# The order of GpSimd's and VectorE's steps around the fp6 quantisers of a transformer-mamba kernel

## The reference, cut to what matters

```python
x = x + attention(layernorm(x), Wqkv, Wproj)          # x: 16 x 1024 x 256, fp32
x = x + ffn(layernorm(x), weight, bias)               # the first quantised layer
x = x + mamba_and_mlp(layernorm(x), ...)
x = x + ffn(layernorm(x), weight, bias)               # the last quantised layer

def ffn(x, weight, bias):                             # both operands go through an fp6 grid
    xq, xs = quantize(x); wq, ws = quantize(weight)   # blocks of 32 along the 256 features
    return (xq * xs) @ (wq * ws).T + bias
def quantize(t):
    scales = maximum(max(abs(block)) / 7.5, 1e-30)
    return nearest_on_grid(block / scales), scales    # grid of fp6 e2m3
```

## Time and profile before

| | |
|---|---|
| median of 3 runs | 9802.43 us (9801.89 to 9803.57) |
| profiled execution, its own time | 9804.51 us |
| its span, first to last instruction | 9802.8 us |
| busy: TensorE | 7878.8 us (80%) |
| busy: VectorE | 7618.6 us (78%) |
| busy: ScalarE | 4259.3 us (43%) |
| busy: GpSimd | 4330.9 us (44%) |
| mean granted TensorE clock | 0.909 |

### The profile page before, as it was taken

One profiled execution on the slowest core, in us unless ns is written; L12 is line 12 of the kernel. 1 busy time (PEld: TensorE's weight loads), 2 busy tenths in 40 slices (PEclk: granted clock), 3 DMA queues, 4 the chain that ended last, 5 costly groups with the idle time before them and its releaser, 6 DMA issues. The chain is left out here.

```text
span 9802.8 us, 98275 instructions
## 1 busy us (share of the span) xinstructions
PE 7878.8 (80%) x31796; PEld 3811.3 (39%) x31796; DVE 7618.6 (78%) x11589; ACT 4259.3 (43%) x7991; POOL 4330.9 (44%) x2631
## 2 busy tenths in 40 slices
PE   5788787887978878788887878878788787887977
PEld 2343343433434334343343434434343243432434
DVE  5787977779687696876878778787787877878777
ACT  2535435254442543525435254353534535345353
POOL 1451825418154271632726336262361724518245
PEclk8898998989989898898989889899898988989989
DMA  3020020200202002020020200102011020100202
GB/s 78 1 51 3 5 49 1 52 1 9 45 0 53 1 9 45 0 53 1 13 41 0 53 1 22 32 0 53 1 28 26 0 53 1 38 15 5 49 1 52
DMA packets 265191, 229.93 MB, mean 23 GB/s; under 512 B 26947, under 2 KB 237635, under 8 KB 264531
## 3 DMA queue, kind: packets, MB, share of 16 engines
q1 hardware_dynamic: 264678, 223.50, 10.6%
HBM read 151.60 MB, written 70.25 MB: 23 GB/s over the span
## 5 line engine op out<-in xcount | busy, mean ns | idle before, releaser
L639 POOL TENSOR_TENSOR arena<-arena 128x1024 f32<-128x1024 f32 x1024 | 2435.6, 2389 | 1312.4 <-DVE arena L1041 862.4
L778 ACT ACTIVATE PS<-arena,Aneg 128x512 f32<-128x512 f32 x2048 | 1410.5, 691 | 1628.1 <-DVE XNT L1081 883.6
L704 ACT ACTIVATE arena<-PS 128x512 f32<-128x512 f32 (+3 forms) x3072 | 1286.9, 508 | 861.4 <-PE PS L1249 856.9
L1363 PE MATMUL PS<-XNT,identf 128*128 128x512 f32 x2048 | 1012.2, 618 | 320.9 <-POOL XNT L622 320.9
L948 DVE TENSOR_REDUCE pm<-PS 128x1 f32<-128x512 f32 (+3 forms) x1728 | 1051.2, 663 | 271.5 <-PE PS L1228 169.6
L601 POOL TENSOR_SCALAR_AFFINE_SELECT arena<-arena 128x512 f32<-128x512 f32 x512 | 329.6, 644 | 2063.6 <-ACT arena L704 2063.6
L1225 PE MATMUL PS<-arena 96*128 96x512 bf16 (+3 forms) x3072 | 1105.5, 385 | 106.3 <-PEq L1447 49.4
L1363 PE MATMUL PS<-arena,identf 128*128 128x512 f32 x2048 | 1025.6, 625 | 161.9 <-DVE arena L1057 161.9
L1249 PE MATMUL PS<-arena 99*128 99x512 bf16 (+3 forms) x3072 | 894.5, 332 | 5.9
L1348 PE MATMUL PS<-arena,sel 96*128 96x512 bf16 x1664 | 513.7, 391 | 389.0 <-DVE arena L1057 319.5
L686 ACT ACTIVATE XNT<-PS 128x512 f32<-128x512 f32 x320 | 187.4, 597 | 1335.2 <-PE PS L1184 1334.5
(11 more groups left out here) (143 smaller groups left out, 13086.2 us busy)
## 6 DMA issues: line engine op xcount, KB each, us to landing
pieces_scratch<-arena SPq DMA_DIRECT2D x816, 64.0 KB
arena<-pieces_scratch SPq DMA_DIRECT2D x68, 384.0 KB, 10.0
arena<-pieces_scratch SPq DMA_DIRECT2D x85, 256.0 KB, 10.5
arena<-in_x SPq DMA_DIRECT2D x17, 1024.0 KB, 5.6
U<-in_x SPq DMA_DIRECT2D x17, 1024.0 KB, 5.6
arena<-pieces_scratch SPq DMA_DIRECT2D x136, 128.0 KB, 10.2
out<-X SPq DMA_DIRECT2D x64, 256.0 KB, 5.7
arena<-pieces_scratch SPq DMA_DIRECT2D x17, 768.0 KB
```

The costliest lines, as they stand in the source:

```text
L639: nc.gpsimd.tensor_tensor(DB[:, n % 2], DTU[:, j, half(th)].unsqueeze(1).to_broadcast([P, SP2, TH]), BB[:, SP2 * sg:SP2 * (sg + 1), :], AL ...
L704: A(PT[s % len(PT)][:, hh, 0:w], bank(t_bank(n))[:, 0:w], ACT.Exp, scale=DH ** -0.5)\
L778: A(bank(da_bank(m)), DT[:, j, half(th)], ACT.Exp, scale=Aneg[:, j, SP2 * sg + ss:SP2 * sg + ss + 1]).then_inc(S("dA"), 1)
L1363: ins = MM(bank(4 + jt % 2), identf[:, :], HS[k % len(HS)][:, ss, :], start=False, stop=sg == NSG - 1 and ss == SP2 - 1)
```

## The change

Three things change. First, the scale is computed by `scalar_tensor_tensor` with a second input, a small constant tile `least` that holds 1e-30, in place of `tensor_scalar` with two constants. Second, in the first quantised layer both halves are centred together, and one call of the quantiser takes all four lanes: the first six steps run over four lanes, the last four steps over two lanes at a time. Third, VectorE raises a new semaphore `quiet` ahead of each group of these last four steps, and GpSimd waits for it: with the bias additions in both layers, and with piece 7 in the last layer. In the first layer the bias is added to all eight tiles by one instruction. In the last layer GpSimd's order becomes piece 7, rescale of pair 0, bias of half 0, rescale of pair 1, `layer_power(2, 1)`, bias of half 1, rescales of pairs 2 and 3.

```diff
+        least = sb("least", [P, 2 * NQB])
-        def quantize(own, rows, lanes):
+        def quantize(own, rows, lanes, at_once=2, quiet=None):
...
-            step(lambda scl, rcp, amx, v, h, a, src: TS(scl, amx, 1.0 / 7.5, 1e-30, ALU.mult, ALU.max))
+            step(lambda scl, rcp, amx, v, h, a, src: STT(
+                out=scl, in0=amx, scalar=1.0 / 7.5, in1=least[:, 0:nb], op0=ALU.mult, op1=ALU.max))
...
-            step(lambda scl, rcp, amx, v, h, a, src: STT(
-                out=a, in0=h, scalar=ROUND, in1=v, op0=ALU.mult, op1=ALU.add))
...
+            for first in range(0, len(lanes), at_once):
+                some = range(first, min(first + at_once, len(lanes)))
+                if quiet is not None:
+                    quiet()
+                step(lambda scl, rcp, amx, v, h, a, src: STT(
+                    out=a, in0=h, scalar=ROUND, in1=v, op0=ALU.mult, op1=ALU.add), some)
...
+                for n in some:
+                    scl, rcp, amx, v, h, a, src = lanes[n]
+                    own.wait(at[n])
+                    yield STT(out=v, in0=h, scalar=-ROUND, in1=a, op0=ALU.mult, op1=ALU.add)
...
+                ch.link(nc.vector.memset(least[:, :], 1e-30))
...
-            def quantized(f, k, th):
-                pool.wait_ge(S("xn"), NT * k + NT // NTH * (th + 1))
-                nc.gpsimd.tensor_tensor(X[:, tiles(th), :], X[:, tiles(th), :],
-                                        bias[:, :].unsqueeze(1).to_broadcast([P, NT // NTH, C]), ALU.add)\
+            def add_bias(after, which, read):
+
+                pool.wait_ge(S("quiet"), after)
+                pool.wait_ge(S("xn"), read)
+                count = which.stop - which.start
+                nc.gpsimd.tensor_tensor(X[:, which, :], X[:, which, :],
+                                        bias[:, :].unsqueeze(1).to_broadcast([P, count, C]), ALU.add)\
                   .then_inc(S("xb"), 1)
-                for p in range(th * NT // 4, (th + 1) * NT // 4):
+
+            def rescale(f, pairs):
+                for p in pairs:
                     pool.wait_ge(S("q"), NT // 2 * f + p + 1)
...
-            quantized(0, 0, 0)
-            quantized(0, 0, 1)
+            add_bias(1, slice(0, NT), NT)
+            rescale(0, range(NT // 2))
...
             layer_power(2, 0)
+            pool.wait_ge(S("quiet"), 3)
             front_pieces(pool, own, range(NT - 1, NT))
-            quantized(1, 2, 0)
+            rescale(1, range(1))
+            add_bias(4, tiles(0), NT * 2 + NT // NTH)
+            rescale(1, range(1, 2))
             layer_power(2, 1)
-            quantized(1, 2, 1)
+            add_bias(5, tiles(1), NT * 3)
+            rescale(1, range(2, 4))
...
-                         quant_place(f, n, 0)) for n in pairs]):
+                         quant_place(f, n, 0)) for n in pairs], NT // 4, lambda: dve.sem_inc(S("quiet"), 1)):
                     ins.then_inc(S("q"), 1)
...
-            quant_half(0, 0, 0)
-            quant_half(0, 0, 1)
-            dve.wait_ge(S("xb"), NTH)
+            for th in range(NTH):
+                centred(0, 0, th)
+            grid(0, range(NT // 2))
+            dve.wait_ge(S("xb"), 1)
...
-            quant_half(1, 2, 1)
-            dve.wait_ge(S("xb"), 2 * NTH)
+            centred(1, 2, 1)
+            grid(1, range(NT // 4, NT // 2))
+            dve.wait_ge(S("xb"), 3)
```

More of the change, by code:

```diff
@@ L248, in blocks, with step @@
                 return t.rearrange("p (n q) -> p n q", q=QB)
-            def step(op):
-                for n, lane in enumerate(lanes):
+            def step(op, which=range(len(lanes))):
+                for n in which:
                     if at[n]:
                         own.wait(at[n])
-                    at[n] = own.did(op(*lane))
+                    at[n] = own.did(op(*lanes[n]))
             TS, STT, TT = nc.vector.tensor_scalar, nc.vector.scalar_tensor_tensor, nc.vector.tensor_tensor
@@ L266, in quantize @@
             step(lambda scl, rcp, amx, v, h, a, src: TS(h, h, 1.0, 1.0 / 16, ALU.max, ALU.mult))
-            step(lambda scl, rcp, amx, v, h, a, src: STT(
-                out=a, in0=h, scalar=ROUND, in1=v, op0=ALU.mult, op1=ALU.add))
[L271 to L277, removed]
+            for first in range(0, len(lanes), at_once):
[4 more added lines that the diff above has]
+                    out=a, in0=h, scalar=ROUND, in1=v, op0=ALU.mult, op1=ALU.add), some)
+                step(lambda scl, rcp, amx, v, h, a, src: STT(
+                    out=src, in0=h, scalar=ROUND + 2, in1=v, op0=ALU.mult, op1=ALU.add), some)
+                step(lambda scl, rcp, amx, v, h, a, src: STT(
+                    out=a, in0=src, scalar=ONE_STEP_DOWN, in1=a, op0=ALU.mult, op1=ALU.min), some)
+                for n in some:
+                    scl, rcp, amx, v, h, a, src = lanes[n]
+                    own.wait(at[n])
+                    yield STT(out=v, in0=h, scalar=-ROUND, in1=a, op0=ALU.mult, op1=ALU.add)
         with nc.Block() as block:
@@ L916, in grid, with centred @@
                         (sc[:, n], rs[:, n], am[:, n], *(quant_place(f, n, m) for m in range(1, 4)),
-                         quant_place(f, n, 0)) for n in pairs]):
+                         quant_place(f, n, 0)) for n in pairs], NT // 4, lambda: dve.sem_inc(S("quiet"), 1)):
                     ins.then_inc(S("q"), 1)
-            def quant_half(f, k, th):
+            def centred(f, k, th):
                 centre(th, lambda i: quant_rows(f, i // 2)[:, i % 2, :])
                 dve.wait_ge(S("xn"), NT * k + NT // NTH * (th + 1))
-                grid(f, range(th * NT // 4, (th + 1) * NT // 4))
             def joint_rows(th):
@@ L1122, in vector_program @@
                 if n == NMLP - 4:
-                    centre(0, lambda i: quant_rows(1, i // 2)[:, i % 2, :])
-                    dve.wait_ge(S("xn"), NT * 2 + NT // NTH)
+                    centred(1, 2, 0)
                 if n in (NMLP - 4, NMLP - 3):
```

## The result

The changed kernel takes 9861.84 us (median of 4 runs, 9857.94 to 9865.47), the kernel before 9802.6 us: a ratio of 1.0061, with a 95% interval of 1.0048 to 1.0074. It is slower by 59 us. The forecast was 9883 us, slower by 81.

What follows compares the result with a forecast made beforehand. VectorE's own queue was taken to set the end of both quantisers. First layer +2.52 us and last layer +2.55 us gave +5.07 us per element, times 16 81 us, so 9883 us, with a range of 9845 to 9915.

Steps and rivals of the forecast that it cites:

- VectorE bounds both stretches: Both quantisers of one element: VectorE's own queue sets the end, busy 24.13 of 24.20 us and 28.56 of 29.40 us.
- the two-input steps are not quiet: Four last quantiser steps: scalar_tensor_tensor contends with GpSimd like tensor_tensor, held up to the whole remainder less 0.14 us.
- Rival A: Four last steps not held at all by GpSimd: net -6.0 us per element, 9706 us, faster; chance 0.13.
- What it removes: Holds on scale, reciprocal product and centring all go: 7.06 us per element, 3.67 in the first layer, 3.39 in the last.
- First layer, the bias: One 128 x 2048 GpSimd addition gets in among the four last steps and holds VectorE 4.37 us.
- rival C: Dense steps keep GpSimd out until their stream ends: net +6.6 us per element, 9908 us; chance 0.06.
- The sign that I had named for C: A GpSimd addition in the trace that takes far longer than 4.6 us.
- Last layer: Holds of 1.52 us by piece 7 and 4.42 us by two biases, less 3.39 us removed: +2.55 us per element.
- The rule of the remainder less 0.14 us: A held VectorE step waits for what is left of the GpSimd instruction less 0.14 us, read from L261.
- What is late next: TensorE's products and last rescale behind the first layer, and last-layer stores: taken as 0, TensorE bounds -0.8 and +1.0 us.
- The sum: Both layers together +5.07 us per element, 16 times that 81 us: 9883 us, slower by 0.8%.
- Theory T: Expectation for two follow-up runs: element period moves only in whole 3.4 us steps; 9803 or 9858 us, then 9748 or 9694.

Runs made afterwards that it cites:

- e_last: Kernel before with the changed order in the last layer alone, keeping the constant tile for the scale: 9806.10 us, ratio 1.0004.
- e_best: Kernel before, with first-layer halves both centred first, then quantised half after half, and bias added in pieces beside one-input work or PSUM reads: 9698.63 us, ratio 0.9892.
- e_dial: Kernel before with two added, unused VectorE reductions ahead of the first layer's centring: 9802.54 us, ratio 1.0001.
- e_late: Changed kernel with quiet raised one step later, behind the first of the four last steps: 9914.76 us, ratio 1.0115.
- e_halves: Changed kernel with the first layer quantised half after half in two lanes, one bias addition per half behind its own raise of quiet: 9807.29 us, ratio 1.0016.
- e_four: Changed kernel, four lanes kept, first-layer bias of half 0 added beside the reductions and that of half 1 behind the rescales: 9806.77 us, ratio 1.0004.
- e_split: Changed kernel with the first layer's 128x2048 bias addition made two of 128x1024: 9861.17 us, ratio 1.0060.
- e_early: Changed kernel with quiet raised one step earlier, ahead of the second one-input step: 9862.31 us, ratio 1.0061.
- e_gap: Changed kernel with VectorE waiting for its own last instruction ahead of the four last steps: 9872.14 us, ratio 1.0069.
- e_first: Kernel before with the changed order in the first layer alone, keeping the constant tile for the scale: 9876.95 us, ratio 1.0074.

## Why the prediction was right, and where it was not

**VectorE bounds both stretches, and the two-input steps are not quiet.** Right for the kernel before; in the changed first layer VectorE then sat idle for 9.37 us, so its queue no longer set the end. `scalar_tensor_tensor` was held wherever GpSimd got in ahead of it: 2.02 us by a bias addition (forecast 2.21), 0.29 and 0.84 us by piece 7 (forecast 1.52 together), and as the scale in `e_last` 1.06 us. Rival A, no hold at all, is refuted by the L275 of 2.71 us.

**What it removes.** Right: the forecast was 7.06 us for each element, and by the means of the groups the scale, L263 and the centring became 7.15 us shorter together.

**First layer, the bias.** This step was wrong. I wrote that GpSimd gets its turn even in a dense stream, from L560 among the L878, and took a hold of 4.37 us on VectorE. Instead GpSimd was kept out for 10.7 us, which is the mechanism of rival C. The L878 read one tensor; I carried what they allow over to steps with two. The sign that I had named for C, an addition far longer than 4.6 us, is there, and the stretch that I had put at 26.7 us took 20.31. The addition and the rescales came behind the stream, as C had it, and the first layer grew by 5.4 us, not 2.5 and not C's 7.6. C's bill took TensorE's products at the slow rate of the earlier trace rows (5.74 us); they took 4.49 and 3.72 us.

**Last layer.** The mechanism was right and the terms near, except that the second half's addition found VectorE at L268 and held that one-input step (2.90 us in place of 0.76), not one of the four last. The stretch to the last step grew by 1.73 us, against 2.55. The holds came to 5.3 us against 5.94. The rule of the remainder less 0.14 us stands (L275 found 2.16 us of L597 left and was held 2.02), but each GpSimd instruction had already run 0.1 to 0.5 us when VectorE's next step asked, which I had not taken off.

**What is late next.** I took 0 for TensorE's tail with bounds of -0.8 and +1.0; it gave back 0.87 us in the last layer. I had not looked for it in the stages that nobody edited, where another 2.9 us came back.

**The sum.** By the stretches the two layers cost 6.25 us more, against my 5.07; the element grew by 3.4. So 9862 us lies in the range, between forecast and no change, because two errors partly cancelled: a dearer mechanism in the first layer, and time that TensorE returned. The direction was forecast for a reason that held in the last layer alone, and that the size came near was luck. The range was also added up loosely: 19 us on either side of 9870 and 9899 gives 9851 to 9918, not 9845 to 9915.

**Steps of 3.4 us.** Except in `e_best`, lengths did not add up. The period of an element can be read from one GpSimd instruction that runs once in each. The rows give its count, shortest, middle and longest duration in ns, and its first and last start in us, for the kernel before, the changed one, `e_dial`, `e_late` and `e_best`:

```profile
L651 POOL TENSOR_TENSOR X<-X,U x16: 4504/4510/4521, 625.2 to 9687.6; 128x2048 f32<-128x2048 f32 x16
```

```profile
L664 POOL TENSOR_TENSOR X<-X,U x16: 4501/4507/4517, 631.5 to 9745.5; 128x2048 f32<-128x2048 f32 x16
```

```profile
L651 POOL TENSOR_TENSOR X<-X,U x16: 4500/4504/4516, 624.7 to 9686.9; 128x2048 f32<-128x2048 f32 x16
```

```profile
L664 POOL TENSOR_TENSOR X<-X,U x16: 4507/4511/4516, 629.6 to 9794.3; 128x2048 f32<-128x2048 f32 x16
```

```profile
L656 POOL TENSOR_TENSOR X<-X,U x16: 4500/4505/4520, 622.4 to 9582.4; 128x2048 f32<-128x2048 f32 x16
```

Divided by 15 these are 604.2, 607.6, 604.1, 611.0 and 597.3 us. Single elements are nearly all at one of these: `e_last`, `e_halves` and `e_four` at 604.2, `e_split` and `e_early` at 607.6, `e_gap` at 607.6 eleven times and 611.0 four times. `e_first` alone also has elements between (607.6, 608.1, 610.4, with a mean of 608.9; the 610.8 in what I expected of `e_dial` was one of its elements). The levels are 3.4 us apart, or 55 us over 16 elements. The two runs of `e_halves` at 9860 us are one such step above its other eight. Apart from `e_first`, whatever a change did to a stretch, nearly every element ended on one of these levels, and in the two stretches looked at the difference came with TensorE's granted clock. Theory T left two results open for each of two runs. `e_dial` came out at one of its two (no change), where adding lengths gave 9825 us. `e_best` came out at one of its two as well (597.3 us), but since its lengths add up to the same time, it doesn't tell the theories apart. What makes the levels was not tried.

**What stays open.** In every case a gap in VectorE's stream let GpSimd in, and a two-input step ready behind another kept it out. Behind a one-input step it got in with two lanes (`e_halves`, last layer) and with four (`e_early`), but not in the first layers of the changed kernel, `e_first`, `e_split`, `e_gap` and `e_late`, where in four lanes the request came during an L268 with another L268 ready. No run tells why.

## What to carry to other kernels

Before moving GpSimd's work beside VectorE's, sort VectorE's instructions by what the trace shows them doing beside a GpSimd instruction. Here reductions ran free (two L257 in 1.28 us), and so did `add_scaled`, which reads one input from PSUM (0.48 us in `e_best`). Steps with two inputs in SBUF did not (L275, 2.71 us in place of 0.69), and neither did the one-input `tensor_scalar` (L268, 2.90 us in place of 0.76). Then ask which engine loses: with small gaps in its stream VectorE waited for the rest of the GpSimd instruction, and in a gapless stream of two-input steps GpSimd waited for the end of the stream, and so did what was queued behind it. And where a loop's clocked engine absorbs small differences, time a change at the whole loop and try it at more than one size before believing or dismissing it.

## What the runs showed of the hardware that was not expected

- GpSimd can be kept out by VectorE for as long as two-input instructions follow without a gap: 10.7 us in the changed first layer, 5.2 us for a rescale in `e_gap`, 4.5 us with two lanes in `e_late`. The Trainium skill, page "SBUF — State Buffer", section "Who interferes with whom", has the one that issues second blocked until the other finishes; in the changed first layer the request waited while 20 VectorE instructions finished, so there the measurement decides.
- A gap of 0.03 us, as between the single-lane steps of the last layer or behind one wait in `e_gap`, was enough to turn that round: there the first L276 was held 4.2 us and the addition took 5.54 us in place of 15.18.
- The period of this loop of 604 us moved in levels 3.4 us apart in 11 of 12 kernels, and TensorE's granted clock changed with it in the two stretches shown (0.80 to 0.82 and 0.89 to 0.91). What makes the levels is open.
